# ScalarE stages a half's rows before it copies the next edges, and GpSimd splits the wait of a group's eight scatters

## What is computed

```python
msg_in = jnp.concatenate([x[row], x[col], edge_attr], axis=-1)
h = msg_in @ W + b
mu = jnp.mean(h, axis=-1, keepdims=True)
var = jnp.mean(jnp.square(h - mu), axis=-1, keepdims=True)
h = (h - mu) * jax.lax.rsqrt(var + LN_EPS) * gamma + beta
msg = jax.nn.relu(h)
out = jax.ops.segment_sum(msg, row, num_segments=x.shape[0])
...
x = _layernorm(x + out, axis=-1)
```

## Time and profile before

| | us |
|---|---|
| median of 3 runs | 1757.65 |
| the profiled execution | 1758.61 |
| its span, first to last instruction | 1756.8 |
| PE / PEld / DVE / ACT / POOL busy | 1201.1 / 1049.7 / 949.3 / 711.4 / 771.9 |

### The profile page before, as it was taken

How to read it: one execution, slowest core, us unless ns; L and a number is a source line. 1 busy time by engine, 2 the same in 40 slices (tenths; PEclk the granted TensorE clock), 3 DMA queues, 4 the chain that set the end, 5 groups by cost and what they waited for, 6 DMA issues and landing times.

```text
span 1756.8 us, 36181 instructions
## 1 busy us (share of the span) xinstructions
PE 1201.1 (68%) x9913; PEld 1049.7 (60%) x9914; DVE 949.3 (54%) x2787; ACT 711.4 (40%) x2814; POOL 771.9 (44%) x810
## 2 busy tenths in 40 slices
PE   6598776666766666766666666667666667656775
PEld 5455666655666556666566666566555656655662
DVE  7623355545555445554455555455455455538997
ACT  3223343433434333443334333344344344335766
POOL 0335544455444455444554444554445554450003
PEclk9767777878878788787888778788888777878998
DMA  7665455344443444444444443444444444312322
GB/s 213 170 129 137 127 154 147 111 127 131 129 115 116 124 131 129 120 115 125 126 130 130 115 128 113 131 130 127 112 120 126 131 128 128 111 54 80 92 65 73
DMA packets 192458, 215.22 MB, mean 123 GB/s; under 512 B 51350, under 2 KB 141802, under 8 KB 192272
## 3 DMA queue, kind: packets, MB, share of 16 engines
q1 hardware_dynamic: 166236, 160.39, 35.1%
q0 software_dynamic: 25088, 51.83, 8.5%
q10 hardware_dynamic: 948, 0.79, 0.2%
HBM read 144.85 MB, written 68.06 MB: 121 GB/s over the span
## 4 chain that ended last, share of the span: by engine, by line
PE 39%; another core or an unknown queue 24%; issue 18%; ACT 10%; DVE 6%; DMA 2%; DVEq 1%; SPq 0%; ACTq 0%
PE bank L962 11%; PE bank L940 7%; PE bank L916 7%; ACT late L1183 5%; PE bank L856 5%; PE bank L930 3%; PE bank L969 2%; ACT turn L1145 1%; DVE late L1580 1%; PE bank L846 1%; DMA tabB<-room 1%; PE bank L844 1%; ACT late L1189 1%; DVEq L493 1%
## 5 line engine op out<-in xcount | busy, mean ns | idle before, releaser
L683 POOL DMA_INDIRECT rows<-p,pos_idx x784 | 756.0, 964 | 825.3 <-ACT p L1149 535.0
L1145 ACT COPY turn<-bank 128x512 f32<-128x512 f32 x196 | 115.0, 587 | 688.0 <-remote 523.3
L962 PE MATMUL bank<-wc,turn 128*128 128x128 f32 x1552 | 297.2, 351 | 66.9 <-ACT turn L1145 59.9
L940 PE MATMUL bank<-room 128*128 x2592 | 246.4, 250 | 106.6 <-issue 61.4
L962 PEld LDWEIGHTS bank<-wc,turn 128*128 128x128 f32 x1552 | 257.4, 251 | 88.1 <-ACT turn L1145 79.3
L940 PEld LDWEIGHTS bank<-room 128*128 128x128 bf16 x2592 | 204.3, 115 | 128.0 <-issue 117.6
L1183 ACT ACTIVATE late<-room 128x128 f32<-128x128 f32 x864 | 256.4, 303 | 2.7 <-issue 1.3
L916 PE MATMUL bank<-late 128*128 128x129 f32 x1472 | 230.3, 299 | 33.9 <-issue 31.4
L1580 DVE SCALAR_TENSOR_TENSOR late<-room,late,floor 128x128 f32<-128x128 f32 x864 | 248.1, 349 | 0.4 <-issue 0.3
L916 PEld LDWEIGHTS bank<-late 128*128 128x128 f32 x1472 | 207.5, 214 | 26.4 <-issue 26.0
L1175 ACT COPY room<-bank 128x512 bf16<-128x512 bf16 x216 | 127.0, 588 | 223.9 <-remote 128.8
(11 more groups left out here) (240 smaller groups left out, 1256.1 us busy)
## 6 DMA issues: line engine op xcount, KB each, us to landing
p<-in_edge_attr_dram SPq DMA_DIRECT2D x98, 512.0 KB
room<-rows SPq DMA_DIRECT2D x256, 129.0 KB
near_bc<-near SPq DMA_DIRECT2D x98, 256.0 KB
late<-rows SPq DMA_DIRECT2D x176, 129.0 KB
rows<-p,pos_idx POOLq DMA_INDIRECT x784
win<-tabB SPq DMA_DIRECT2D x196, 31.5 KB
rows<-fill SPq DMA_DIRECT2D x24, 193.5 KB
tabB<-room SPq DMA_DIRECT2D x12, 384.0 KB, 3.8
```

Source lines behind the costliest of these rows:

```text
L683: nc.gpsimd.indirect_dma_start(rows_ap, bass.IndirectOffsetOnAxis(pos_idx[:, k, j:j + 1], 0), stage[:, k, j, :], None).then_inc(st_free[k] ...
L940: mm = pe.matmul(bank[A_BANK + b2][:, jj * D:(jj + 1) * D], selT[b2][:, jj * P:(jj + 1) * P], tabA[:, bass.ds(at[jj // UJ], 1), part, :], ...
L962: pe.matmul(bank[H_BANK + h][:, t * D:(t + 1) * D], eT[h][:, t * P:(t + 1) * P], wc[:, 2, :], start=(t == 0), stop=False, skip_group_check ...
L1145: nc.scalar.copy(eT[h], bank[E_BANK][:]).then_inc(eT_ready, 1)
```

## The change

On ScalarE, from the second group on, `stage_rows` of the half before moves from behind `squares` to ahead of `copy_edges`, and `number_rows` moves from the second half of a group, behind `copy_edges`, to the end of its first half. On GpSimd, the first four scatters of a group no longer wait for the second half's staged rows, but for its products (`h_done`) and for the first half's rows; ahead of the fifth scatter it waits for the second half's rows. The first group has no wait for the products.

```diff
-            def scatter(g, k):
+            def scatter(g, k, windowed=False):
                 pool.wait_ge(pos_ready, g + 1)
                 pool.wait_ge(lo_ready, g + 1)
-                early = isinstance(g, int) and g == 0
-                pool.wait_ge(st_ready, 2 * g + (1 if early else 2))
+                pool.wait_ge(st_ready, 2 * g + 1)
+                if windowed and not (isinstance(g, int) and g == 0):
+                    pool.wait_ge(h_done, 2 * g + 2)
                 settle()
                 for j in range(COLS):
-                    if early and j == COLS // 2:
-                        pool.wait_ge(st_ready, 2)
+                    if j == COLS // 2:
+                        pool.wait_ge(st_ready, 2 * g + 2)
+                        settle()
                     nc.gpsimd.indirect_dma_start(rows_ap, bass.IndirectOffsetOnAxis(pos_idx[:, k, j:j + 1], 0),
                                                  stage[:, k, j, :], None).then_inc(st_free[k], 16)
...
-                every_group(lambda g, k, u: scatter(g, k))
+                every_group(lambda g, k, u: scatter(g, k, True))
...
                         s, c, q, r = pair_of(g, h)
+                        if h == 1 and g > 0:
+                            stage_rows(g, k, 0)
+                        elif h == 0 and g > 0:
+                            stage_rows(g - 1, slot(k, -1), 1)
                         copy_edges(g, h)
+                        if h == 1 and not g > 0:
+                            stage_rows(g, k, 0)
                         t = 2 * g + h
                         if A_AT < t <= A_AT + NQ:
                             a_mid(t - A_AT - 1)
-                        if h == 1:
-                            number_rows(g, k, u)
                         if not below(s, 1, 0):
                             copy_selT(s, c)
                         if not below(s, 0, 0):
                             squares(s, c)
-                        if h == 0 and not below(g, 0, 1):
-                            stage_rows(g - 1, slot(k, -1), 1)
-                        if h == 1:
-                            stage_rows(g, k, 0)
                         if not below(s, 0, 0):
                             roots(s, c)
+                        if h == 0:
+                            number_rows(g, k, u)
```

## The result

The changed kernel takes 1812.15 us (median of 4 runs, 1807.02 to 1819.13), the kernel before 1756.97 us beside it (4 runs, 1753.57 to 1757.97): **ratio 1.032, interval 1.028 to 1.036, slower**. The profiled execution after took 1807.02 us. Against the profiled one before (1758.61) that is +48.4 us.

The account below looks back on a forecast made before the run. Bound: a chain of waits, not an engine. +0.5 us a group (0.65 + 0.05 - 0.2) over 87 groups, +43, less 5.5 at the end, takes 1758.6 to 1796, median 1795 us; 8-in-10 range 1670 to 1845, forecast's own 1765 to 1830.

Parts of the forecast that it names:

- The chain behind the release: Staging copy, edge copy, low-clock products, then scatter after each release: +0.8 us a group, +0.3 with the staging copy out of the way.
- the release: Moment, 1.8 us after a group's last scatter is issued, when TensorE's held signals reach ScalarE and VectorE.
- The clock: TensorE's clock high at the release: products 1.2 us earlier, in one group of five, so -0.2 us a group.
- The late signal passes in the burst: First half's selector, turned at t = 2.4 after the first scatter, is still received while the group's scatters run.
- the burst: The eight scatters of one group on GpSimd; t = 0 is its beginning.
- much slower: Rival: selector's signal held to the release, leaving the second half's work behind it; +2.9 us a group, 2005 us; chance 0.06.
- The first 11 groups: Groups outside the 87 that share their halves with the second pass; the forecast gave them no cost.
- The end: Last two bursts no longer join, so VectorE goes on sooner after the last products: 5.5 us gained.
- The new wait in the middle: GpSimd's wait before the fifth scatter is already met when reached; its own cost taken as 0.05 us a group.
- Faster, by signals that get through: Rival: high clock at each release gives 1692 us, a freeze also 1 us shorter 1605; chance 0.32.
- the freeze: Time in a burst when TensorE's finished work does not reach ScalarE and VectorE; may depend on SyncE's loads.
- all of it comes at once at the release: Claim that all of TensorE's held signals arrive together at t = 11.6, 1.8 us after the last scatter is issued.

Follow-up runs that it names:

- e12: Kernel before, with ScalarE's staging copy of the second half moved up right behind the edge copy; third chip, signals late: 1884.55 us, ratio 1.0829.
- e8: Changed kernel, with ScalarE's staging copy and VectorE's add made to wait until the previous group's scatters land; second chip: 1840.74 us.
- e9: As e8, but each half's staging copy comes right behind the edge copy instead of ahead of it; second chip: 1805.12 us.
- e5: The whole change, unaltered, against the kernel before on the second chip: 1245.28 us against 1249.23, ratio 0.9978.
- e1: Kernel before with only the change's ScalarE order, GpSimd's waits left as before; first chip: 1247.05 us against 1245.95, ratio 1.0004.
- e10: As e9, but all eight scatters wait for both halves' staged rows, as before the change; third chip: 2122.21 us, ratio 1.2203.
- e7: Kernel before, with ScalarE's edge copy and VectorE's add made to wait until the scatters two groups back land; second chip: 1784.15 us.
- e6: Changed kernel with five small GpSimd instructions (3.2 us) between the fourth and fifth scatter; second chip: 1500.94 us, ratio 1.2035.

## Why the prediction was right

**The chain behind the release: right, and its size.** Forecast +0.8 us where the clock is low: 16.2 us a group; measured 16.25 (mean; median 16.22), +0.67 against 15.58. The terms are in the trace: the edge copy 0.48 us late (forecast 0.48 to 0.57), L964 0.64 us after its start, 2.50 us of products, 0.95 to the scatter (0.91). The release is at t = 11.8 in the mean of both kernels. The staging copy stands ahead of the edge copy at 77 of 83 releases, where I had two in three. Most of the 0.13 between 0.8 and 0.67 is that the mean of before is 15.58 and the row that I worked from 15.4.

**The clock: its share was mis-sized, and the sum held by luck.** I gave the high clock one group in five at 1.2 us, -0.2. At 23 of 83 releases L964 takes under 1.3 us (median period 15.17, 1.05 under the low clock's median of 16.22), and at 18 more the clock rises inside it (1.31 to 1.59 us, median period 15.45). Worked out from these medians, that alone would be an estimated -0.5. But among these 41 groups are four of the five in which the selector's signal was held to the release, so their mean gain is 0.62, which makes -0.3. The sum per group was to be +0.5; it is +0.36 over 85 periods, +31 us where +43 was forecast for 87.

**The late signal passes in the burst: right in 78 of 83 groups.** Turned by t = 1.7, received at 4.3 in the group shown, by 8.7 in all of the 78. In the other five "much slower" is what happened, for that group alone: 17.1 to 19.6 us. As a whole the rival fell, but e12 shows that it was no idle one, at 1885 us.

**The first 11 groups: the failed step.** "This holds for the 87 groups that share their halves with the second pass" left the others at zero; they cost +19.4 us. What the trace shows in its place is a chain that is longer by the second half's products in groups 4 to 10 (+16.0), and a pause of 11.6 us in group 3, which the shorter periods of the first three groups make good for two thirds (+3.4 for groups 0 to 3). In e8 and e9 it is +29 and +30.

**The end: the step right, the gain not.** From the last products to VectorE's add it is 12.41 us in place of 18.05, -5.6 for a forecast of -5.5. But I had taken the last products to come at the same place. Before, they were done 4.7 us after the start of the last burst but one; with the change a release and its chain stand ahead of them, and they are done at 14.7. The last period (+5.4) and what follows the last burst (-4.7) together are +0.7 us.

**The new wait in the middle** costs nothing that can be seen in the steady groups: the fifth scatter is 1.26 us behind the fourth, as the others. In the first 11 groups GpSimd stands idle at it for 11.6 us (group 3), 3.3 (group 6) and 1.6 (group 8).

**Faster, by signals that get through: not here.** On two other chips they do get through, and there the whole change (e5) is worth nothing that can be told: 0.9978, 0.9945 to 1.0011. One form of this rival, that the freeze depends on what SyncE loads in the burst, is answered by the result's own trace: the edge load (L515) moved from t = 2.8 (median) to 11.8 and the DMAs' rate in the first 4 us of a burst fell from 188 to 90 GB/s, but the release stayed at 11.8.

**The sum.** Of the profiled execution, 1807.02 us where 1796 was forecast, the miss of 11 is +19.4 (first groups), +6.2 (end), -12.2 (steady groups) and -2.6 (setup). So the total is nearer than its parts. The median lies 5 us above the profiled execution, which makes it 17 us over the forecast's 1795.

## What to carry to other kernels

The start of a long operation that holds others up is two things at once: the end of the chain that it waits for, and the moment that closes the door on what comes next. Shortening the chain ahead of it by 1.5 us cost 146 us here (e12), because the next half's edges then came too late to get across. That is one kernel with this hold-up, and no general price. So before a start is moved, list for every engine what will have been signalled by that moment before and after the move; the longest step that falls to the other side is the price, at the clock that the engine then has. And look at the stages without the usual partner (here the first 11 groups) by a row of their own.

## What the runs showed of the hardware

The hold-up is not a property of the kernel alone. Two chips ran the kernel before in 1242 to 1249 us (medians); it took 1757 us in the result's runs and 1739 on the third chip, with the same instructions in the same order and scatters of equal length (mean 973 ns in e1, 964 before). Whether it belongs to the chip or to the occasion is not shown: only the second chip was visited twice, about 20 minutes apart, both times without it. In the burst of e12 shown above TensorE's signals take 5.3 and 7.0 us to arrive: `select_a` ends at 744.64 and its add starts at 749.95, the turned edges are ready at 745.76 and copied at 752.79. So they are late by a time, in order, and not held to one instant: "all of it comes at once at the release" was too strict, though it gave the chains of both kernels. Nor is the time a smooth one. In the trace after, the selector copy in the burst starts near t = 3.6 (8 groups), 4.3 (10), 5.8 (16), 7.2 (25) and 8.6 (6), and in only 13 of the 78 groups elsewhere. What holds the signals up, and why they come in such steps, no run shows.

One more thing goes with it. Each scatter counts up a semaphore 16 times as its parts land, 3200 counts for two of the four semaphores and 3072 for the others. The traces of the two chips without the hold-up have 2915 to 3190 a semaphore as single events. The traces of before and after have 451 to 637, those of e10 to e12 728 to 1370. So where TensorE's signals come late, many of the scatters' counts too are not recorded one by one. Whether both have one cause no run here shows.

The landing of a burst (from the end of the last scatter's issue to its last count) goes with the pause behind the burst more than with the chip: its median is 3.4 to 3.5 us in e1 to e5, where the bursts follow each other, and on chips of the same kind 2.4 in e7, 1.5 in e8 and e9 and 1.3 in e6, where they don't; 1.2 in the traces of before and after. The Trainium skill (DMA: Bandwidth & Descriptors, "Anatomy of one DMA") states some 2.0 us for the fixed part of such a DMA. The medians, which do not count the 0.96 us of the issue, lie on either side of it. In the 11.6 us pause of group 3 signals do pass: L786 ends at 115.89 and VectorE goes on at 115.93, 5.7 us after the fourth scatter. In the shorter pause of group 6 too: L871 ends at 175.96 and ScalarE goes on at 176.00, 1.4 us after the end of the fourth scatter's issue. And in group 8 one passes at once inside the burst: L871 ends at 208.94, ScalarE goes on at 208.98, while the fourth scatter (208.28) is being issued. What a pause does in the steady groups, with the second pass beside them, no run shows.
